# ACT's tap copies as fp32 pairs, and the splits of a group ahead of them

## The reference

```python
q, k, v = (einsum('blh,dh->bdl', u, W) + b for each of Wq, Wk, Wv)
k  = causal_conv(k, k_kernel) + k_D * k        # first convolution, 512 taps a channel
kv = k * v
y  = causal_conv(kv, ssm_kernel) + D * kv      # second convolution
y  = einsum('blc,oc->blo', swap(y * q), Wo) + bo
x  = layernorm(u + y)
h  = square(relu(x @ W_fc.T))
x  = layernorm(x + spikes(h @ W_proj.T) / 5)   # spikes: 5 steps, as thresholds
```

## Time and profile before

| what | value |
|---|---|
| median of 3 runs | 903.79 us (903.4 to 907.43) |
| profiled execution, its own time | 906.38 us |
| its span in the trace | 904.2 us |
| busy share of the span: PE, DVE, ACT, POOL | 83%, 88%, 57%, 46% |
| mean granted clock of TensorE | 0.949 |

### The profile page before, as it was taken

How to read it: one execution, slowest core, us unless ns; L and a number is a source line. 1 busy time by engine, 2 the same in 40 slices (tenths; PEclk the granted TensorE clock), 3 DMA queues, 4 the chain that set the end, 5 groups by cost and what they waited for, 6 DMA issues and landing times.

```text
span 904.2 us, 26707 instructions
## 1 busy us (share of the span) xinstructions
PE 749.5 (83%) x11392; PEld 549.7 (61%) x11392; DVE 799.9 (88%) x1164; ACT 516.5 (57%) x560; POOL 416.1 (46%) x307
## 2 busy tenths in 40 slices
PE   0077879888888988856559999999999999999993
PEld 0077879888888987855435555555545555555541
DVE  6895859999999999999756899999999999999885
ACT  2384656766666766743325665655656555666562
POOL 0331212333333322322337866667876666886542
PEclk9997979999999999977679999999999999999997
DMA  9984859888888787676110011111011111011001
GB/s 338 336 213 123 190 140 211 196 192 201 191 191 186 181 195 158 135 154 188 48 40 7 1 47 46 47 47 45 2 46 46 46 46 46 14 33 47 24 24 46
DMA packets 55579, 101.01 MB, mean 112 GB/s; under 512 B 5728, under 2 KB 41440, under 8 KB 53600
## 3 DMA queue, kind: packets, MB, share of 16 engines
q1 hardware_dynamic: 54144, 97.94, 42.0%
q10 hardware_dynamic: 1376, 2.23, 0.7%
HBM read 89.92 MB, written 27.01 MB: 129 GB/s over the span
## 4 chain that ended last, share of the span: by engine, by line
DVE 30%; PE 22%; POOL 22%; issue 21%; ACT 2%; DMA 1%; POOLq 0%; SPq 0%; DVEq 0%; ACTq 0%
POOL arena L671 13%; DVE arena L1229 7%; PE ps L858 5%; PE ps L747 5%; PE ps L725 5%; PE ps L865 4%; POOL arena L631 4%; POOL arena L636 3%; DVE arena L1073 2%; DVE u_maxima L959 2%; DVE arena L1186 2%; DVE arena L1226 2%; PE ps L839 2%; DVE arena L1205 2%; DVE arena L1211 1%
## 5 line engine op out<-in xcount | busy, mean ns | idle before, releaser
L510 ACT ACTIVATE arena<-arena 64x3584 f16<-64x3584 f16 x60 | 191.2, 3189 | 114.6 <-DVE arena L1053 113.9
L725 PE MATMUL ps<-arena 128*128 128x96 f16 x3072 | 144.1, 211 | 74.9 <-DVE arena L1012 51.6
L725 PEld LDWEIGHTS ps<-arena 128*128 128x128 f16 x3072 | 139.3, 101 | 77.8 <-issue 51.1
L747 PE MATMUL ps<-arena 128*128 128x64 f16 (+2 forms) x5088 | 148.4, 184 | 45.2 <-POOL arena L631 28.8
L671 POOL TENSOR_TENSOR arena<-arena 128x512 f16<-128x512 f32 x128 | 178.9, 1429 | 14.7 <-ACT arena L554 14.2
L865 PE MATMUL ps<-arena 128*128 128x512 f16 x768 | 173.1, 379 | 2.8 <-POOL arena L671 2.8
L747 PEld LDWEIGHTS ps<-arena 128*128 128x128 f16 x5088 | 145.1, 99 | 48.3 <-POOL arena L631 20.5
L858 PE MATMUL ps<-arena 128*128 128x512 f16 x768 | 170.8, 379 | 0.9 <-issue 0.9
L636 POOL TENSOR_TENSOR arena<-arena 128x512 f16<-128x512 f32 x32 | 47.8, 1492 | 255.3 <-ACT arena L516 255.3
L1218 DVE TENSOR_TENSOR arena<-arena 128x512 f32<-128x512 f32 x128 | 137.6, 1128 | 10.4 <-POOL arena L671 9.0
L550 ACT ACTIVATE arena<-ps,read_factor 128x512 f32<-128x512 f32 x128 | 87.9, 687 | 78.6 <-PE ps L858 62.0
(11 more groups left out here) (107 smaller groups left out, 848.7 us busy)
## 6 DMA issues: line engine op xcount, KB each, us to landing
arena<-kpad_dram SPq DMA_DIRECT2D x166, 256.0 KB, 5.1
kpad_dram<-ksplit_dram SPq DMA_DIRECT2D x64, 256.0 KB, 6.0
qy<-in_uT SPq DMA_DIRECT2D x8, 1024.0 KB, 17.3
arena<-in_u SPq DMA_DIRECT2D x16, 512.0 KB, 4.0
out<-arena SPq DMA_DIRECT2D x16, 512.0 KB, 3.0
qy<-kpad_dram SPq DMA_DIRECT2D x22, 256.0 KB, 6.3
arena<-in_k SPq DMA_DIRECT2D x2, 512.0 KB, 4.8
ksplit_dram<-arena ACTq DMA_DIRECT2D x2, 512.0 KB, 3.7
```

The costliest lines, as they stand in the source:

```text
L510: nc.scalar.activation(*shifted(windows1_of(s, half)), ACT.Copy).then_inc(c1_copied, 1)
L725: last = nc.tensor.matmul(o, u16[:, x, t, tok:tok + P], wcur[:, w, t], start=(k == 0), stop=(k == 3 * DT - 1))
L747: last = nc.tensor.matmul(out[:, ch * COL + delta * B:(ch + 1) * COL], win[:, delta * P:(delta + 1) * P], data(xp, ch)[:, 0:cols], start=( ...
```

## The change

ACT's copy of the shifted taps is made on the same bytes seen as fp32, so that one element is two fp16 values. In step g ACT makes the two splits first (kv of g, keys of g + 1) and then both copies of group g + 1; the copies of groups 0 and 1 are made ahead of the steps. `causal` is no longer built in place by POOL: POOL builds it in `step_st`, which lies in the first columns of `kv16`, and ACT copies it from there in the same fp32 form. DVE's own copies (L1060, L1073, L1077) stay as they are, and so does which engine copies what.

```diff
+        step_st = kv16[:, 0, 0, 0:P]
...
+            def as_pairs(dst, src):
+                return dst.bitcast(F32), src.bitcast(F32)
+
+            act.wait_ge(id_done, 2)
+            nc.scalar.activation(*as_pairs(causal, step_st), ACT.Copy).then_inc(causal_done, 1)
             act.wait_ge(scales1, 1)
...
             def copy_windows(s, g, half):
 
                 act.wait_ge(c1_masked, 2 * g + half + 1)
-                nc.scalar.activation(*shifted(windows1_of(s, half)), ACT.Copy).then_inc(c1_copied, 1)
+                nc.scalar.activation(*as_pairs(*shifted(windows1_of(s, half))), ACT.Copy).then_inc(c1_copied, 1)
 
             def step(s, g):
-                if g + 1 < NG:
-                    copy_windows(s + 1, g + 1, 0)
                 act.wait_ge(kv_ready, g + 1)
                 nc.scalar.activation(kv16[:, s % 2, 0], vbuf[:, s // GPC, group_of(s):group_of(s) + GC], ACT.Copy
                                      ).then_inc(kv_hi, 1)
                 if g + 1 < NG:
                     k_part(g + 1)
-                if g + 1 < NG - GPC:
+                if 0 < g < NG - 1:
+                    copy_windows(s + 1, g + 1, 0)
+                if 0 < g < NG - GPC - 1:
                     copy_windows(s + 1, g + 1, 1)
 
             for half in range(2):
                 copy_windows(0, 0, half)
             k_part(0)
+            for half in range(2):
+                copy_windows(1, 1, half)
...
-            nc.gpsimd.memset(causal, 1.0).then_inc(id_zero, 1)
+            nc.gpsimd.memset(step_st, 1.0).then_inc(id_zero, 1)
...
-            nc.gpsimd.affine_select(out=causal, in_=causal, compare_op=ALU.is_ge, fill=0.0,
+            nc.gpsimd.affine_select(out=step_st, in_=step_st, compare_op=ALU.is_ge, fill=0.0,
...
-            dve.wait_ge(id_done, 2)
+            dve.wait_ge(causal_done, 1)
```

More of the change, by code:

```diff
@@ L215, in build @@
             sem(n) for n in ("t_zero", "c1_masked", "c2_masked", "c1_copied", "c2_copied"))
-        c1_copied_dve, c1_half, c2_half, c2_widened = (
-            sem(n) for n in ("c1_copied_dve", "c1_half", "c2_half", "c2_widened"))
+        c1_copied_dve, c1_half, c2_half, c2_widened, causal_done = (
+            sem(n) for n in ("c1_copied_dve", "c1_half", "c2_half", "c2_widened", "causal_done"))
         ld_wcur, ld_wnext, wcur_ready = (sem(n) for n in ("ld_wcur", "ld_wnext", "wcur_ready"))
```

## The result

| | before | after |
|---|---|---|
| median of 4 runs | 903.74 us | 883.32 us |
| span in the trace | 904.2 us | 881.1 us |
| DVE busy | 799.9 us | 770.7 us |
| ACT busy | 516.5 us | 424.8 us |
| POOL busy | 416.1 us | 391.7 us |

The ratio to the kernel before is 0.9766, 95% interval 0.9735 to 0.9797. The forecast was 881.5 us with a range of 872 to 893. A second series on another occasion gave 883.51 us, ratio 0.9778 (0.9753 to 0.9802). The medians are 20.4 us apart and the two spans 23.1 us, since the profiled execution of the kernel before was 2.6 us longer than its median.

What follows compares the result with a forecast made beforehand. DVE was taken as the bound. Gains of 16.0 us (142 to 305 us), 5.5 (305 to 397) and 1 (397 to 441) sum to 22.5, a span of 881.7 from 904.2; forecast 881.5 us, range 872 to 893.

Steps and rivals of the forecast that it cites:

- the steady stretch: From 142 to 305 us, 15 groups: 17.3 us gained at 9.7 us each, less 1.3 for the lower clock: 16.0.
- the start: Before 142 us: PE's own stalls set the pace and ACT was already early, so 0 us gained.
- the groups from 20 to 27: From 305 to 397 us, 8 groups: same collision, at most 1.3 us each, 10.4 in all; 5.5 us taken.
- the tail: From 397 to 441 us, without projections: between 0 and 3 us gained, 1 taken.
- ACT's order: Steady groups: kv split about 0.8 us after `times_v`, POOL's pair ended by about 3.9; period 9.44 us, every fourth 10.0.
- The copies as pairs: ACT's 60 tap copies as fp32: 1.7 us each instead of 3.19, saving 90 us of ACT's time, all hidden.
- the step "half": From 305 to 397 us: not all of 10.4 us can be had, given window and issue waits; half, 5.5.
- the step matrix: One 128x64 ACTIVATE at the head of ACT's queue, where ACT was idle: cost 0.
- another limit takes most of it: Rival: DMA at 97% queues, DVE waits for windows, steady period held at 10.2 us; 891.5 us, chance 0.18.
- more than forecast: Rival: no jitter in the steady stretch, full gain in the 8 groups after 305 us; 871.3 us, chance 0.12.
- The slower case: Rival: ACT's paired copies are slow, from 3.6 us each the gain is gone; at 4.0, 925 us; chance 0.06.
- that of no change: Rival: PE's loop is nearer 10.8 us than 9.44, say by a lower clock; 903 us, chance 0.04.

## Why the prediction was right

The mechanism was right and is shown. That the total came within 2 us is in part luck: the steady stretch gave 3.0 us more than its term, the start 1.75 more, the groups from 20 to 27 3.9 less and the tail 0.2 less, which nearly cancels, to 23.1 us of span for 22.5.

**ACT's order.** Right, to hundredths. 0.78 us to the split, 3.89 to POOL's end, 2.22 and 1.05 us on DVE, 9.44 us as the period by PE's loop, and 9.98 in the fourth group where I had 10.0. (The masks there take 1.55 us and not 1.13, but end 4.9 us after `times_v` as summed.) A group of the kernel before in which ACT happened to be early was a complete model of the kernel after.

**The steady stretch.** Worth 19.0 us, where the sum had 16.0. The two terms by which I went below the chains were not there: I took 9.7 us for the mean of 9.58, for jitter between two equal chains and a full DMA, and it was 9.59 at a DMA share of 0.97. And I gave back 1.3 us for the lower clock, but the clock was 1.00 in the stretch. Before, it had one piece at the lower level there, from 182 to 192 us, behind a wait of PE of 1.31 us, and after the change PE waits at most 0.5 us at a time. That the shorter waits kept the clock up is not shown.

**The copies as pairs.** 1.695 us each where I took 1.7, and 91.7 us of ACT's time hidden. But "the shorter form buys cover and no time" is wrong. With the order alone the total is 889.9 us, about 7 more. I had found the second copy 0.3 us late and let it go; in a loop that PE closes, 0.3 us in every group counts, and in the fourth groups, where the copies start 3.3 us after `times_v` and not 2.0, it was 1.1 us. The step left out the multiplication by the groups.

**Groups 20 to 27.** 1.6 us where the sum had 5.5, and all of it from group 20, which is still in PE's loop. For the written-out groups the step "half" was wrong: DVE was 7.7 us shorter there and the time did not move. What I named grew in its place. The waits of the changed kernel from 284 to 375 us:

```profile
PE ps L756 <- issue: 8.7, 10, 2.0
PE ps L734 <- issue: 4.4, 5, 1.4
...
DVE arena L1062 <- DMA arena<-kpad_dram: 2.6, 2, 1.9
...
DVE qy L1062 <- DMA qy<-kpad_dram: 1.4, 1, 1.4
```

PE's issue waits grew from 4.8 us before (4.2 of it in the earlier trace rows) to 13.1, and DVE's for windows from the 1.11 of the earlier trace rows to 4.0. The run with PE's loop cut short shows that written-out code alone brings such issue waits. How the missing gain divides between issue waits, windows and clock is open. So is why these seven groups take nearly the same time, 78.6 to 82.5 us, in every kernel here, the one with the added subtraction too.

**Before group 5.** 1.75 us where I had 0. Group 0 took 11.05 us for 12.23. That is not shown to be the change's doing: the same kernel took 10.73 in the second series, and others with ACT's new order took 10.94 to 12.25. The first `times_v` started at 80.22 us for 80.57, so the step matrix shows no cost, as I had it.

**The tail.** 0.8 us where I had 1.

**The rivals.** That another limit takes most of it fell at 9.59 us a group with DMA at 0.97. That there is more than forecast held for the steady stretch and failed after it, on the issue waits. The slower case fell with 1.695 us a copy, and that of no change with the rest. In the latter I gave PE 9.1 us of work a group; the earlier trace rows have 142.44 / 15 = 9.5, and the changed kernel measured 9.3.

## What to carry to other kernels

When an idle engine's work order decides when POOL starts, it also decides what on DVE the POOL work meets: place it beside DVE's reads of PSUM, not its fp16 copies in SBUF. Look in the trace before for a group where the new order already happened by chance; here its period, 9.44 us, was that of the loop. Ask stage by stage what the freed engine will wait for next: here seven groups with 7.7 us less work for DVE gained nothing. And a lateness of a few tenths on an engine that closes the loop is to be multiplied by the groups before it is called nothing.

## What the runs showed of the hardware

- A POOL subtraction of 128x512 and DVE's fp16 copies exclude each other both ways: in the run with the added one, the copy pair took 3.18 for 2.22 us and the subtraction 2.12 for 1.16. DVE's 128x384 copy did the same (0.96 for 0.25 us). DVE's reads of PSUM beside POOL stayed at 0.68 and 0.74 us. The Trainium skill (SBUF — State Buffer, Who interferes with whom) says that DVE's copies can run in two-port modes, which share a pair of ports with POOL, and that whoever issues first holds this pair for the whole instruction. It also says that a DVE instruction with two inputs in SBUF contends with a POOL instruction that reads SBUF. The copies agree with the first, and the masks, 1.05 for 0.47 us, with the second.
- The same PE instructions written out instead of looped cost 12.2 us over seven groups, with 9.9 us marked issue between 210 and 300 us and 17 packets on the instruction queue q8. In the loop, from 200 to 284 us, the changed kernel had no issue wait of PE and no packet on that queue.
- In the 143.8 us with DMA at a busy share of 0.97 no wait of an engine is put down to a DMA.
